# Order of TensorE's work over the last two batches of a cross-attention, causal self-attention and mixture-of-experts layer

## The chip, the cores and the metric

The kernel runs on 1 core of one Trainium2 chip. The metric is the device time of one execution in microseconds (us), median of several runs. Before the change it is 362.99 us (3 runs, 362.04 to 364.71).

## What is computed

One transformer layer in float32 over x of shape (4, 128, 512), that is 4 batches of 128 tokens, with a context of (4, 2048, 384). The reference, cut to its steps:

```
x = x + cross_attention(layernorm(x), ctx, Wq, bq, Wk, bk, Wv, bv)      # one head of 512
n = layernorm(x)
cq  = layernorm(n @ W_dq)  * g + b ;  Q = cq @ W_uq
ckv = layernorm(n @ W_dkv) * g + b ;  K, V = split(ckv @ W_ukv)
s = tril(Q K' / sqrt(32)), exact zeros become -inf                       # 16 heads of 32
x = x + softmax(s) V  W_o'
n = layernorm(x)
routed = sum over 4 of 16 experts of w_e * relu(n U_e')^2 D_e'
shared = relu(n SU')^2 SD'                                              # inner width 1024
x = x + routed + shared
```

## The kernel before

Everything is written out by hand, one instruction stream for each engine, tied by semaphores. The context is read in 16 chunks of 512 keys (4 for each batch), and the main loop goes over steps: scores of a chunk, its exponential, its transpose and its product with the context, each some steps behind the other. The later stages of a batch (attended values, the middle layer norm, the compressed queries and keys, the self-attention, the output projection) are woven into the steps of the batches behind it. After the last step comes a tail in which nothing of the chunk loop is left to lay between, written as a plain list of calls on each engine. The change is in TensorE's list there. The names in it:

- `sums_T(b)`, `attended(b)`: the cross-attention's result of batch b, transposed and multiplied with Wv.
- `rows_T(n, bank)` (L1589): four transposes of a normalised batch into a bank of PSUM. "middle" is the norm ahead of the self-attention, "last" the one ahead of the experts. ScalarE then copies the bank's rounded high part (`rows_hi`, L745), VectorE the rest (`rows_lo`, L1084), since each product is made of three rounded products (`split_mm`, L1582 to L1584). An instruction of it has 128x128 weights and as many columns as the other operand is wide.
- `compress(b)`, `compressed_T(b)` (L1773), `keys_and_queries(b)` (L1785), `values(b)` (L1791): the projections of the self-attention. Between the first two VectorE makes moments and a normalisation (`moments_2`, `normalise_2`, with the root on GpSimd, L620).
- `pair_scores(u)` (L1732): scores of units u and u+1. A unit is 4 heads of a batch; there are 16 units (`UNITS`), 4 for each batch. VectorE then masks and takes maxima (`find_masked`, `put_lowest`, `highest`: L1092, L1096, L1100), ScalarE takes the exponential (`unit_exp`, L852), VectorE inverts the sums, GpSimd scales (`unit_weights`, L627), `unit_T(u)` (L1742) transposes on TensorE, ScalarE copies out (`unit_copy`, L841), and `unit_sums(b)` (L1801) multiplies with the values of a batch. `hs_bank(u)` gives the bank of a unit's scores: from unit 8 on they are banks 6, 4 and 0 by turns, unit 13 being the last one in bank 0. `pair_scores(u)` waits until the exponential of unit u-2 has been taken.
- `project(b)`: the output projection of batch b. VectorE adds it (`self_added`, L1328) and the last norm follows. `router(b)`: the gate's 16 columns for a batch.
- `first_up(e, m)`: up product of shared block e (0 or 1), column half m, for the first two batches at once, by `up_half(e, 0, m)`: 12 instructions of 256 columns each. `half_bank(e, h)` says into which bank. ScalarE takes `relu_half(e, 0)` and `squared_half(e, 0)`, VectorE `gated_half(e, 0)`. `first_down(e, b)` are the down products. Afterwards `up_half(e, 1, m)` makes the up products of the last two batches, and `up(2, counts)` those of block 2, with `counts` (L1967 to L1971), the first product that needs the routing, between. `entries` (L1979) is the second.

The orders on the other engines that matter: ScalarE has `unit_exp(9)`, `attended_hi(1)`, `down_hi(0)`, `down_hi(1)`, `unit_exp(10)`, `compressed(3)` in this row, and at the end `unit_copy(15)`, `relu_half(0, 0)`, `attended_hi(3)`, `squared_half(0, 0)`, `rows_hi` of batch 2, `router_exp(2)`, `relu_half(1, 0)`. VectorE has `rows_lo` of batch 3, `find_masked(10)`, `put_lowest(10)`, `attended_lo(1)`, `moments_2(3)`. Then, after the last `rows_lo`, comes `down_lo(2)`, the routing (its selection is L1164), the gate weights (L1170 to L1183), and the table of entries (to L1215).

Of the kernel before, what the change touches and what calls it, by code (L numbers as in the profile page):

```python
# [25 lines left out]
P = 128  # L26
# [10 lines left out]
def layer_program(nc, x, ctx_in, ctxT_in, wqT, wkT, wv, wd, wu, woT, experts, bq, bk, bv, gate, bias_e,  # L37
                  gammas_betas, out):
    NB, S, D = x.shape
    NKEY, TD = ctx_in.shape[1:]  # L40
    DC = D // P
# [12 lines left out]
    IC = 2  # L54
# [24 lines left out]
    with ExitStack() as es:  # L79
# [38 lines left out]
        xT_h = sb("xT_h", [P, DC, T], F32R)  # L118
        xT_l = sb("xT_l", [P, DC, T], F32R)
# [110 lines left out]
        def u_part(e, i):  # L230

            return u_w[e][:, i, :]
# [48 lines left out]
        def small(name, shape, dt=F32):  # L281
# [36 lines left out]
        bank = [es.enter_context(nc.psum_tensor(f"bank{i}", [P, 512], F32)) for i in range(8)]  # L318
# [16 lines left out]
        var_ok, rstd_ok, xn_ok, xT_mm, xhi_ok, xlo_ok = (sem(n) for n in ("var_ok", "rstd_ok", "xn_ok", "xT_mm", "xhi_ok", "xlo_ok"))  # L335
# [7 lines left out]
        qkv_mm, qkv_ok, hs_mm, hnb_ok, exp_ok, hrd_ok, hw_ok, hwT_mm, hwT_ok, a_mm, ahi_ok, alo_ok, wo_mm, x2_ok = (sem(n) for n in (  # L343
            "qkv_mm", "qkv_ok", "hs_mm", "hnb_ok", "exp_ok", "hrd_ok", "hw_ok", "hwT_mm", "hwT_ok", "a_mm", "ahi_ok", "alo_ok", "wo_mm", "x2_ok"))
        lg_mm, rexp_ok, sel_ok, cnt_mm, cnt_ok, ent_ok, ent_mm, idx_ok = (sem(n) for n in (
            "lg_mm", "rexp_ok", "sel_ok", "cnt_mm", "cnt_ok", "ent_ok", "ent_mm", "idx_ok"))
        up_mm, relu_ok, sq_ok, g_ok, acc_mm, base_ok, y_out = (sem(n) for n in (
            "up_mm", "relu_ok", "sq_ok", "g_ok", "acc_mm", "base_ok", "y_out"))
# [10 lines left out]
        ulo_first, dlo_first = sem("ulo_first"), sem("dlo_first")  # L359
# [6 lines left out]
        def tok(b):  # L366
            return slice(b * S, (b + 1) * S)
# [10 lines left out]
        UNITS = NB * ROWS  # L378
# [3 lines left out]
        B_S, B_W, B_O, B_POST, B_A = 2, 3, 4, 5, 7  # L382


        B_ACC, B_UP = (1, B_O, B_A, B_S), ((B_POST, 0), (6, B_W))

        def rows_bank(b):

            return 1 if b < NB - 1 else B_S
# [8 lines left out]
        HT_TOK = T // 2  # L398
# [3 lines left out]

        def half_bank(e, h):

            return B_UP[e][0] if h else B_POST

        def half(h):
            return slice(h * HT_TOK, (h + 1) * HT_TOK)
# [34 lines left out]
        norm_no = {(kind, b): NB + i for i, (_, kind, b) in enumerate(order)}  # L443
# [1133 lines left out]
        def _(pe):  # L1577
            mm = nc.tensor.matmul

            def split_mm(dst, a, b, start, stop):  # L1580

                mm(dst, a[0], b[1], start=start, stop=False)  # L1582
                mm(dst, a[0], b[0], start=False, stop=False)  # L1583
                return mm(dst, a[1], b[0], start=False, stop=stop)  # L1584

            def rows_T(n, dst):
                pe.wait_ge(xn_ok, n + 1)
                for c in range(DC):
                    last = nc.tensor.transpose(dst[:, c * P:(c + 1) * P], xn[:, n % 2, c * P:(c + 1) * P], ident[:])  # L1589
                last.then_inc(xT_mm, 1)  # L1590
# [34 lines left out]
            for h in range(DC):  # L1625
                for i in range(2):
                    last = mm(bank[B_ROW][0:2, 0:TDB], bq2[:, h, :], wk2[:, i, h, :], start=h == 0 and i == 0, stop=h == DC - 1 and i == 1)
# [65 lines left out]
            def up_half(e, h, m):  # L1693
# [7 lines left out]
                if m == IC - 1:  # L1701
                    last.then_inc(up_mm, 1)

            def first_up(e, m):
                pe.wait_ge(xlo_ok, norm_no["last", 1] + 1)
                if e == 0:
                    pe.wait_ge(qkv_ok, 3 * NB - 1)
                else:
                    pe.wait_ge(relu_ok, e)
                up_half(e, 0, m)  # L1710

            def first_down(e, b):
                pe.wait_ge(dlo_first, 2 * e + 2)
                pe.wait_ge(g_ok, e + 1)
                if e == 0:
                    pe.wait_ge(rexp_ok, NB - 1)
                    pe.wait_ge(exp_ok, UNITS)
                down_tile(e, b, first=e == 0)

            def pair_scores(u):  # L1720

                b, r = divmod(u, ROWS)
                pe.wait_ge(qkv_ok, 3 * b + 2)
                if u > 2 * ROWS:
                    pe.wait_ge(exp_ok, u - 1)
                elif u >= 2:
                    pe.wait_ge(exp_ok, u)
                for j in range(HT):
                    for i in range(2):
                        rows = slice((r + i) * DH, (r + i + 1) * DH)  # L1730
                        o = slice(j * P, (j + 1) * P)
                        last = mm(bank[hs_bank(u + i)][:, o], qk_s[rows, 0, o], qk_s[rows, 1, o], start=True, stop=True)  # L1732
                last.then_inc(hs_mm, 2)

            def unit_T(u, step=TAIL):
                pe.wait_ge(hw_ok, u + 1)
                if step - LAG < G:
                    pe.wait_ge(wT_ok, step - LAG + 1)
                else:
                    pe.wait_ge(hwT_ok, u)  # L1740
                for j in range(HT):
                    last = nc.tensor.transpose(bank[B_W][:, j * P:(j + 1) * P], hw_of(u)[:, j * P:(j + 1) * P], ident[:])  # L1742
                last.then_inc(hwT_mm, 1)
# [49 lines left out]
            def unit_sums(b):  # L1793
                pe.wait_ge(hwT_ok, ROWS * b + ROWS)
                pe.wait_ge(qkv_ok, 3 * b + 3)
                if b >= 1:
                    pe.wait_ge(alo_ok, b)
                for j in range(HT):
                    for r in range(ROWS):
                        h = j * ROWS + r  # L1800
                        last = mm(bank[B_A][r * DH:(r + 1) * DH, j * P:(j + 1) * P], v_s[:, b % 2, h * DH:(h + 1) * DH],  # L1801
                                  hwT(b * ROWS + r)[:, j * P:(j + 1) * P], start=True, stop=True)
                last.then_inc(a_mm, 1)
# [15 lines left out]
            def router(b):  # L1819
                pe.wait_ge(xlo_ok, norm_no["last", b] + 1)  # L1820
                for c in range(DC):
                    last = split_mm(bank[rows_bank(b)][:, 0:NE], (xT_h[:, c, tok(b)], xT_l[:, c, tok(b)]),
                                    (gate_h[:, c, :], gate_l[:, c, :]), c == 0, c == DC - 1)
                last.then_inc(lg_mm, 1)
# [37 lines left out]
            for step in range(1, TAIL):  # L1862
# [22 lines left out]
                if 0 <= g < G:  # L1885
                    b, c = divmod(g, NCH)
# [22 lines left out]
            unit_T(6)  # L1909
            router(0)  # L1910
            unit_T(7)
            rows_T(norm_no["middle", 3], bank[B_POST])
            pair_scores(10)
            unit_sums(1)
            compress(3)
            project(1)
# [6 lines left out]
            unit_T(10)  # L1923
            pe.wait_ge(rexp_ok, 1)
            rows_T(norm_no["last", 1], bank[rows_bank(1)])
            pair_scores(14)
            unit_T(11)
            router(1)
            unit_sums(2)
            unit_T(12)  # L1930
            for m in range(IC):
                first_up(0, m)
            unit_T(13)
            project(2)
            unit_T(14)
            unit_T(15)
            unit_sums(3)
            rows_T(norm_no["last", 2], bank[rows_bank(2)])
            for m in range(IC):
                first_up(1, m)  # L1940
            project(3)
            router(2)
            first_down(0, 1)
            first_down(0, 0)
            rows_T(norm_no["last", 3], bank[rows_bank(3)])
            first_down(1, 1)
            router(3)
            first_down(1, 0)

            for e in range(FIRST):  # L1950
                pe.wait_ge(relu_ok, FIRST)
# [203 lines left out]
```

## Time and profile before

| | us |
|---|---|
| median of 3 runs | 362.99 (362.04 to 364.71) |
| the profiled execution | 367.77 |
| span of its trace | 366.0 |
| TensorE busy | 342.7 (94%) |
| VectorE busy | 241.0 (66%) |
| ScalarE busy | 189.1 (52%) |
| GpSimd busy | 94.9 (26%) |
| mean granted TensorE clock | 0.967 |

All starts in the text are in us from the start of the span. PE is TensorE's matmul, DVE VectorE, ACT ScalarE, POOL GpSimd. The clock is a share of full speed: 1.00 is 2.4 GHz, 0.50 is 1.2 GHz. The listed duration of a matmul overlaps with the next one's, so its price in a row of matmuls is the distance of two starts.

### The profile page before, as it was taken

What the parts mean: (1) busy time and instruction counts of PE and PEld (TensorE: products, weight loads), DVE (VectorE), ACT (ScalarE), POOL (GpSimd) and SP (SyncE); (2) the same over time, 40 slices, a digit from 0 to 9 for tenths busy, and PEclk for the clock granted to TensorE, in tenths of its full rate; (3) what the DMA queues carried; (4) which work ended last, traced back from release to release, by engine and by line L of the source; (5) the groups of instructions that cost most, each with busy time, mean ns of one, the idle gap of its engine ahead of it and who ended that gap; (6) DMA issues with size and microseconds to landing.
All of it is one profiled execution on the core that took longest, in us unless ns stands there. A gap on an engine that the chain in (4) does not pass through costs nothing.

```text
span 366.0 us, 6994 instructions
## 1 busy us (share of the span) xinstructions
PE 342.7 (94%) x2530; PEld 239.9 (66%) x2530; DVE 241.0 (66%) x475; ACT 189.1 (52%) x428; POOL 94.9 (26%) x114
## 2 busy tenths in 40 slices
PE   6999799999999989998879889999998999999996
PEld 4887567677677757766669779887643444444344
DVE  2875978746588377576782468880534677778587
ACT  2547574635566574484754452502134677777520
POOL 3600500000012011443472140004336554432000
PEclk9999999999999999996977998989999999999999
DMA  6982689976222345071050460699834453331573
GB/s 234 402 360 99 236 339 422 375 244 223 86 88 87 107 166 218 29 277 69 3 193 10 144 258 1 243 376 411 318 108 154 148 175 120 126 107 57 202 288 115
DMA packets 17185, 69.70 MB, mean 190 GB/s; under 512 B 2816, under 2 KB 3328, under 8 KB 14592
## 3 DMA queue, kind: packets, MB, share of 16 engines
q1 hardware_dynamic: 12768, 56.93, 41.4%
q0 software_dynamic: 3520, 11.54, 9.2%
q10 hardware_dynamic: 864, 0.79, 0.7%
q8 instruction: 21, 0.34, 0.4%
q14 instruction: 12, 0.10, 0.1%
HBM read 61.91 MB, written 7.34 MB: 189 GB/s over the span
## 4 chain that ended last, share of the span: by engine, by line
PE 74%; DVE 12%; ACT 6%; issue 3%; DMA 2%; another core or an unknown queue 1%; POOL 1%; ACTq 0%; DVEq 0%
PE bank L1582 9%; PE bank L2030 9%; PE bank L2062 9%; PE bank L1584 9%; PE bank L1583 9%; PE bank L1892 8%; PE bank L1999 2%; DMA raw<-in_wkT 2%; PE bank L2073 2%; PE bank L2041 2%; PE bank L1732 2%; DVE cT L1283 2%; PE bank L1785 2%; PE bank L1742 1%; PE bank L1837 1%
## 5 line engine op out<-in xcount | busy, mean ns | idle before, releaser
L1892 PE MATMUL bank<-ring,wT 128*128 128x384 f32 x128 | 44.0, 487 | 0.7 <-ACT wT L894 0.7
L2030 PE MATMUL bank<-WX,xsT 128*32 128x256 f32 (+1 forms) x256 | 38.0, 380 | 0.9 <-DVE xsT L1492 0.9
L2062 PE MATMUL bank<-WX,hsT 128*32 128x512 f32 (+1 forms) x128 | 38.2, 598 | 0.0
L1283 DVE TENSOR_TENSOR cT<-ring_T,cT 128x512 fp32r<-128x512 f32 x45 | 31.0, 732 | 6.6 <-ACT cT L752 6.6
L1892 PEld LDWEIGHTS bank<-ring,wT 128*128 128x128 f32 x128 | 23.6, 190 | 14.2 <-ACT wT L894 0.9
L2030 PEld LDWEIGHTS bank<-WX,xsT 128*32 128x32 f32 x256 | 17.8, 110 | 22.0 <-issue 11.9
L1514 DVE COPY down_copy<-WX 128x1024 f32 x32 | 21.0, 696 | 15.0 <-PE bank L2062 14.8
L2030 PE MATMUL bank<-up_copy,xsT 128*32 128x256 f32 x384 | 30.7, 379 | 0.0
L2062 PE MATMUL bank<-down_copy,hsT 128*32 128x512 f32 x192 | 30.7, 598 | 0.0
L752 ACT CAST cT<-ring_T 128x512 fp32r<-128x512 f32 x48 | 27.0, 618 | 6.5 <-PE bank L1584 6.3
L688 POOL DMA_INDIRECT xs<-x_rows,from_row x20 | 19.6, 982 | 40.7 <-DVE to_row L1237 27.3
L598 POOL TENSOR_TENSOR rstd<-var,mhalf 128x1 f32<-128x1 f32 x12 | 7.5, 625 | 75.0 <-DVE var L1069 74.9
L1507 DVE COPY up_copy<-WX 128x1024 f32 x32 | 21.1, 695 | 8.3 <-remote 3.2
L695 POOL DMA_INDIRECT y_rows<-ys,to_row x16 | 17.1, 1072 | 35.7 <-ACT ys L1000 35.7
L1024 ACT COPY down_copy<-WX 128x1024 f32 x16 | 16.8, 1051 | 18.2 <-PE bank L2062 18.2
L1492 DVE COPY xsT<-bank 128x512 f32<-128x512 f32 x20 | 13.7, 684 | 17.8 <-PE bank L1999 17.6
L1582 PE MATMUL bank<-cT,qk_h 128*128 128x512 f32 x48 | 20.2, 420 | 2.4 <-DVE cT L1283 1.7
L1584 PE MATMUL bank<-cT,qk_l 128*128 128x512 f32 x48 | 18.9, 393 | 0.0
L1583 PE MATMUL bank<-cT,qk_h 128*128 128x512 f32 x48 | 18.8, 392 | 0.0
L1016 ACT COPY up_copy<-WX 128x1024 f32 x16 | 16.7, 1044 | 4.1 <-remote 2.4
L2062 PEld LDWEIGHTS bank<-WX,hsT 128*32 128x32 f32 x128 | 7.4, 109 | 16.4 <-issue 16.4
L1582 PE MATMUL bank<-xT_l,u_w 128*128 128x256 f32 (+1 forms) x48 | 17.8, 370 | 0.0
(296 smaller groups left out, 901.3 us busy)
## 6 DMA issues: line engine op xcount, KB each, us to landing
WX<-in_experts SPq DMA_DIRECT2D x16, 1024.0 KB, 6.0
ring_T<-in_ctxT SPq DMA_DIRECT2D x16, 768.0 KB, 7.1
ring<-in_ctx SPq DMA_DIRECT2D x16, 768.0 KB, 5.2
WX<-y_rows SPq DMA_DIRECT2D x4, 1024.0 KB, 8.2
raw<-in_experts SPq DMA_DIRECT2D x3, 1024.0 KB, 5.0
raw<-in_wqT SPq DMA_DIRECT2D x4, 256.0 KB, 5.7
res<-in_x SPq DMA_DIRECT2D x4, 256.0 KB, 8.2
raw<-in_woT SPq DMA_DIRECT2D x1, 1024.0 KB, 4.8
```

Of the source, the lines that this page charges most:

```text
L688: nc.gpsimd.indirect_dma_start(out=xs[:, s % NXS, :], out_offset=None, in_=x_rows, in_offset=bass.IndirectOffsetOnAxis(ap=from_row[:, s:s ...
L695: nc.gpsimd.indirect_dma_start(out=y_rows, out_offset=bass.IndirectOffsetOnAxis(ap=to_row[:, s:s + 1], axis=0), in_=ys[:, s % NYS, :], in_ ...
L752: copy(cT[:, g % 2, 0, t, :], ring_T[:, g % RING_T, t, :]).then_inc(cThi_ok, 1)
L1283: V_.tensor_tensor(cT[:, g % 2, 1, t, :], ring_T[:, g % RING_T, t, :], f32(cT[:, g % 2, 0, t, :]), ALU.subtract).then_inc(cTlo_ok, 1)
L1507: V_.tensor_copy(up_copy[place(g, q)][:], WX[:, bass.ds(expert * (2 * HALF), HALF)]).then_inc(up_copied, 1)
L1514: V_.tensor_copy(down_copy[place(g, q)][:], WX[:, bass.ds(expert * (2 * HALF) + HALF, HALF)]).then_inc(down_copied, 1)
L1582: mm(dst, a[0], b[1], start=start, stop=False)
L1583: mm(dst, a[0], b[0], start=False, stop=False)
L1584: return mm(dst, a[1], b[0], start=False, stop=stop)
L1892: last = mm(bank[B_O][:, 0:TD], wT[:, g % 2, k * P:(k + 1) * P], ring[:, g % RING, k, :], start=(c == 0 and k == 0), stop=(c == NCH - 1 an ...
L2030: last = mm(bank[B_H[g % 2]][q * SLOT:(q + 1) * SLOT, 0:IC * P], xsT[:, g % 2, c * P + q * SLOT:c * P + (q + 1) * SLOT], w, start=c == 0, ...
L2062: last = mm(bank[B_Y[g % 2]][q * SLOT:(q + 1) * SLOT, :], hsT[:, g % 2, m * P + q * SLOT:m * P + (q + 1) * SLOT], w, start=m == 0, stop=m ...
```

## The change

In TensorE's tail list, and nowhere else:

1. `pair_scores(10)` stands ahead of `rows_T` of batch 3's middle norm.
2. The up products of shared block 0 for the first two batches are cut by batch. `up_rows(0, m, 0)` makes those of batch 0 alone, 12 instructions of 128 columns for each m, and stands between `rows_T` of batch 1's last norm and `pair_scores(14)`. `up_rows(0, m, 1)` stands where `first_up(0, m)` was.
3. `first_up(1, m)` goes into bank 0 (before: bank 5, shared with block 0, so that it waited for block 0's relu). It waits for the exponential of unit 13 instead. Its two halves stand behind `unit_T(14)` and behind `unit_T(15)`; before, both stood behind `rows_T` of batch 2's last norm.
4. `first_down(1, 0)` stands ahead of `router(3)`.

```diff
         def half_bank(e, h):
-            return B_UP[e][0] if h else B_POST
+            return B_UP[e][0] if h else B_UP[0][e]
...
+            def up_rows(e, m, b):
+                for c in range(DC):
+                    o = c * IC * P + m * P
+                    last = split_mm(bank[half_bank(e, 0)][:, m * HT_TOK + b * S:m * HT_TOK + (b + 1) * S],
+                                    (u_part(e, 0)[:, o:o + P], u_part(e, 1)[:, o:o + P]),
+                                    (xT_h[:, c, tok(b)], xT_l[:, c, tok(b)]), c == 0, c == DC - 1)
+                return last
+
             def first_up(e, m):
                 pe.wait_ge(xlo_ok, norm_no["last", 1] + 1)
-                if e == 0:
-                    pe.wait_ge(qkv_ok, 3 * NB - 1)
-                else:
-                    pe.wait_ge(relu_ok, e)
+                pe.wait_ge(exp_ok, UNITS - 2)
                 up_half(e, 0, m)
...
             unit_T(7)
+            pair_scores(10)
             rows_T(norm_no["middle", 3], bank[B_POST])
-            pair_scores(10)
             unit_sums(1)
...
             rows_T(norm_no["last", 1], bank[rows_bank(1)])
+            pe.wait_ge(ulo_first, 2)
+            pe.wait_ge(xlo_ok, norm_no["last", 0] + 1)
+            pe.wait_ge(qkv_ok, 3 * NB - 1)
+            for m in range(IC):
+                up_rows(0, m, 0)
             pair_scores(14)
             unit_T(11)
             router(1)
             unit_sums(2)
             unit_T(12)
+            pe.wait_ge(xlo_ok, norm_no["last", 1] + 1)
             for m in range(IC):
-                first_up(0, m)
+                last = up_rows(0, m, 1)
+            last.then_inc(up_mm, 1)
             unit_T(13)
             project(2)
             unit_T(14)
+            first_up(1, 0)
             unit_T(15)
+            first_up(1, 1)
             unit_sums(3)
             rows_T(norm_no["last", 2], bank[rows_bank(2)])
-            for m in range(IC):
-                first_up(1, m)
             project(3)
...
             first_down(1, 1)
+            first_down(1, 0)
             router(3)
-            first_down(1, 0)
```

The added lines move the line numbers behind them: L1732, L1742, L1801 of before are L1738, L1748, L1807 afterwards. First place, TensorE from `unit_T(7)` (L1742, L1748) to `unit_sums(1)` (L1801, L1807); L1589 is `rows_T` of batch 3, L1732 and L1738 are `pair_scores(10)`. Before:

```order
L1742 MATMUL bank<-ident,hw 128x128 x4
L1589 MATMUL bank<-ident,xn 128x128 x4
L1732 MATMUL bank<-qk_s 128x128 x8
L1801 MATMUL bank<-hwT_first,v_s 32x128
L1801 MATMUL bank<-hwT_odd,v_s 32x128
```

and now:

```order
L1748 MATMUL bank<-ident,hw 128x128 x4
L1738 MATMUL bank<-qk_s 128x128 x8
L1589 MATMUL bank<-ident,xn 128x128 x4
L1807 MATMUL bank<-hwT_first,v_s 32x128
L1807 MATMUL bank<-hwT_odd,v_s 32x128
```

The scores have passed the transposes that wait for VectorE's `xn`. Second place, TensorE from `unit_T(10)` to `unit_T(11)`; L1589 is `rows_T` of batch 1's last norm, L1732 and L1738 are `pair_scores(14)`, `u_w` is the up weight of shared block 0. Before:

```order
L1742 MATMUL bank<-ident,hw_more 128x128 x4
L1589 MATMUL bank<-ident,xn 128x128 x4
L1732 MATMUL bank<-qk_s 128x128 x8
L1742 MATMUL bank<-ident,hw_more 128x128 x4
L1582 MATMUL bank<-gate_l,xT_h 128x16
```

and now:

```order
L1748 MATMUL bank<-ident,hw_more 128x128 x4
L1589 MATMUL bank<-ident,xn 128x128 x4
L1582 MATMUL bank<-xT_l,u_w_72 128x128
L1583 MATMUL bank<-xT_h,u_w_72 128x128
L1584 MATMUL bank<-xT_h,u_w_72 128x128
...
L1738 MATMUL bank<-qk_s 128x128 x8
L1748 MATMUL bank<-ident,hw_more 128x128 x4
L1582 MATMUL bank<-gate_l,xT_h 128x16
```

Eight such triples, 24 instructions of 128 columns, now stand ahead of the last scores. Third place, TensorE from `project(2)` to `project(3)` in the changed kernel, with the banks' numbers: `unit_T(14)`, `first_up(1, 0)`, `unit_T(15)`, `first_up(1, 1)`, `unit_sums(3)`, `rows_T` of batch 2, `project(3)`, each by its first row. Now:

```order
L1748 MATMUL bank3<-ident,hw_more_84 128x128 x4
L1582 MATMUL bank0<-xT_l,u_w1_73 128x256
...
L1748 MATMUL bank3<-ident,hw_more_84 128x128 x4
L1582 MATMUL bank0<-xT_l,u_w1_73 128x256
...
L1807 MATMUL bank7<-hwT_last_68,v_s 32x128
...
L1589 MATMUL bank1<-ident,xn 128x128 x4
L1582 MATMUL bank2<-wo_w_61,aT_last_71 128x512
```

and before, from the same `unit_T(14)` on:

```order
L1742 MATMUL bank3<-ident,hw_more_84 128x128 x8
L1801 MATMUL bank7<-hwT_last_68,v_s 32x128
...
L1589 MATMUL bank1<-ident,xn 128x128 x4
L1582 MATMUL bank5<-xT_l,u_w1_73 128x256
...
L1582 MATMUL bank2<-wo_w_61,aT_last_71 128x512
```

The 24 products of block 1 have gone from between `rows_T` and `project(3)` to behind the two last transposes of units. The lists of the other engines are the same as before.

## Rows read from the trace of the kernel before

**Rows 1.** The page: granted TensorE clock in 40 slices of 9.15 us, in tenths.

```profile
PEclk9999999999999999996977998989999999999999
```

**Rows 2.** Waits of PE, 155 to 260 us: total, times, longest.

```profile
PE bank L1732 <- ACT hw_more L852: 2.4, 1, 2.4
PE bank L1589 <- DVE xn L1079: 1.5, 1, 1.5
...
PE bank L1742 <- ACT hwT_last L841: 0.8, 1, 0.8
PE bank L1582 <- DVE xT_l L1084: 0.7, 1, 0.7
PE bank L1801 <- ACT hwT_odd L841: 0.7, 1, 0.7
```

**Rows 3.** Timeline of PE, 166 to 178 us: start, duration, instruction, idle before.

```profile
166.43 0.92 PE L1589 MATMUL bank<-ident,xn 128*128 128x128 f32 x4 [1.51 <-DVE xn L1079]
167.28 2.08 PE L1732 MATMUL bank<-qk_s 32*128 32x128 f32 x16
169.29 0.42 PE L1801 MATMUL bank<-hwT_first,v_s 128*32 128x128 f32 x1
...
171.15 0.58 PE L1582 MATMUL bank<-DW,xT_h 128*128 128x256 f32 x1
...
176.51 0.44 PE L1773 MATMUL bank<-ident,cqn 128*128 128x128 f32 x2
177.85 2.05 PE L1785 MATMUL bank<-cf,wu_s 128*128 128x128 f32 x16 [0.90 <-ACT cf L861]
```

**Rows 4.** Timelines of ACT and of DVE, 163 to 175 us.

```profile
163.46 0.21 ACT L852 ACTIVATION_READ_ACCUMULATOR hw_more<-bank,hnb 128x1 f32 x1
...
168.00 0.69 DVE L1084 TENSOR_TENSOR xT_l<-bank,xT_h 128x512 fp32r<-128x512 f32 x1 [0.16 <-ACT xT_h L745]
...
173.92 0.50 DVE L1338 BATCH_NORM_STATS2 stats<-bank 128x6 f32<-128x128 f32 x2 [1.25 <-PE bank L1584]
```

**Rows 5.** Windows: stretch, length, busy PE, PEld, DVE, ACT, POOL; granted clock; DMA.

```profile
167.00:173.40 6.40, 6.40 (x60) 5.42 (x59) 3.64 (x7) 3.52 (x11) 2.27 (x2) 0.50 0.01 3
...
187.50:197.20 9.70, 9.70 (x73) 8.97 (x72) 5.40 (x10) 5.95 (x28) 4.08 (x4) 0.50 0.31 120
...
221.50:224.60 3.10, 3.10 (x15) 2.94 (x14) 2.79 (x16) 0.00 (x0) 0.00 (x0) 0.50 0.00 0
```

**Rows 6.** Timelines of PE (and one row of DVE, L1318), 186 to 212 us.

```profile
186.54 1.55 PE L1732 MATMUL bank<-qk_s 32*128 32x128 f32 x16 [2.38 <-ACT hw_more L852]
...
189.43 0.36 PE L1582 MATMUL bank<-gate_l,xT_h 128*128 128x16 f32 x1
189.64 0.36 PE L1583 MATMUL bank<-gate_h,xT_h 128*128 128x16 f32 x1
...
205.36 0.66 PE L1589 MATMUL bank<-ident,xn 128*128 128x128 f32 x4
...
206.12 0.69 DVE L1318 TENSOR_TENSOR aT_last<-bank,aT_last 128x512 fp32r<-128x512 f32 x1 [1.12 <-ACT aT_last L831]
...
206.10 0.28 PE L1584 MATMUL bank<-xT_h,u_w 128*128 128x256 f32 x1
206.21 0.28 PE L1582 MATMUL bank<-xT_l,u_w 128*128 128x256 f32 x1
...
211.59 0.26 PE L1584 MATMUL bank<-gate_h,xT_l 128*128 128x16 f32 x1
```

**Rows 7.** Timelines of PE and DVE, 211 to 242 us.

```profile
211.71 0.26 PE L1582 MATMUL bank<-gate_l,xT_h 128*128 128x16 f32 x1
...
227.35 0.20 DVE L1164 TENSOR_SCALAR r_sel<-r_rank 128x64 f32<-128x64 f32 x1
...
230.30 0.33 PE L1967 MATMUL bank<-r_sel,upper 128*128 128x64 f32 x2
...
239.93 0.48 DVE L1215 TENSOR_TENSOR in_group<-r_eq,cw 128x320 f32<-128x320 f32 x1
...
241.75 3.75 PE L1979 MATMUL bank<-in_group,in_row 128*128 128x40 f32 x32
```

## The prediction

> **What bounds the kernel now.** I read the table of busy times first. TensorE works 94% of the span and the next engine 66%, so time is won only where TensorE stands idle, runs at the low clock, or does less. The clock line of the page comes second [rows 1]: it is at full speed but for the slices from the 19th to the 27th (165 to 247 us), which is where the changed list runs. The waits of TensorE come third [rows 2]: in the tail it waits once for 2.4 us, once for 1.5, and three times for 0.7 to 0.8. The two long ones are the starts at 186.54 and 166.43 in the timeline [rows 6, 3]. The windows come fourth [rows 5]. From 167.0 to 173.4 and from 187.5 to 197.2 TensorE is busy all the time at clock 0.50, that is 1.2 GHz: the two low stretches follow the two long waits by less than a microsecond. A third, 221.5 to 224.6, follows the wait of 0.7 at `router(3)` and that router's instructions of 16 columns. So a wait here costs its own length and a few microseconds at half speed behind it.
>
> The chain of waits goes through VectorE, ScalarE and TensorE by turns until the last scores, and from `router(3)` at 218.84 on TensorE alone is on it. What TensorE gains ahead of that point, the end gains, unless VectorE's routing becomes late.
>
> **Part A, scores ahead of the transposes.** `rows_T` waits for VectorE's `xn` from 164.92 (166.43 less 1.51) on, and the scores of units 10 and 11 stand behind it. Their own condition was met at 163.67, when the exponential of unit 8 was done [rows 4], and their banks 0 and 6 are free with it. They cost 2.01 us at half speed (167.28 to 169.29) [rows 3], so 1.0 at full, and end at about 165.95 inside the wait; `rows_T` starts at 166.43 as before. The wait left is 0.5.
> If the clock falls again at the same place: `rows_T` 0.85, `unit_sums(1)` 1.86 (169.29 to 171.15), then `compress(3)` from 169.14 instead of 171.15. Its 12 instructions take 2.56 at 0.213 each and end at 171.7. `project(1)` behind it begins at half speed (0.46 each), with 3.8 of its 12 instructions before the clock rises at 173.45 and the others at 0.23, and ends at 175.35. `compressed_T` stood right behind `project(1)` at 176.51: 1.16 won. If the clock doesn't fall, `compress(3)` has to wait for `xT_l`, done at 168.69 [rows 4], ends at 170.1, and VectorE's `moments_2` starts some 3.3 earlier than its 173.92; `project(1)` needs VectorE's low part of the attended values, which comes near 170.6, and is done at 173.4: 3.1 won. The two ends are 1.2 and 3.1. Both have rows; I take 2.0. From `compressed_T` to the end of the exponential of unit 12 the chain goes through VectorE's list, which is unchanged and shifts as a whole, GpSimd's and ScalarE's parts with it.
>
> **Part B, the products around the last units**, counted in the times of before, from the end of `rows_T` at 184.16 (186.54 less 2.38) to the end of `project(3)` (208.68 and 12 x 0.232, 211.46).
> - The price of an instruction of 128 columns isn't in the trace. One of 16 columns starts 0.112 to 0.12 after the other at full clock (211.59 to 211.71) and one of 256 columns 0.11 to 0.12 (206.10 to 206.21); at half clock one of 16 takes 0.21 [rows 6, 7]. The width makes no difference between 16 and 256, so one of 128 should be 0.112 as well. The other bound is the float32 product that isn't made of rounded parts: 16 instructions of 128 columns for 8 products in 2.05, 0.256 for a product [rows 3]. I take 0.112, since the same kind of instruction stands on both sides of it. The Trainium skill says (TensorE: Matmul & The Clock Gate, "Step-by-step: what each phase is for") that the time to load the stationary operand scales with its columns and that the load runs beside the matmul ahead of it. By that rule the price is the load's, 0.112 as well, and the rows of 16 and 256 columns agree.
> - Cut by batch, 24 instructions of 256 columns (2.8) become 48 of 128 (5.4): 2.6 more work.
> - The first 24 take 2.7 and fill the wait of 2.38: −2.38, and the last scores come 0.3 late, which is in the 2.6.
> - `first_up(1, m)` fills the waits of 0.8 and 0.7 at `unit_T(15)` and `unit_sums(3)`: −1.45.
> - It no longer stands between `rows_T` of batch 2 and `project(3)`. That projection needs the low part of the attended values, which was there at 206.81, 1.45 after `unit_sums(3)` was through at 205.36 [rows 6]. With only `rows_T` (0.42) between, TensorE waits 1.0. Behind it stand router, down products, and all that follows. +1.0.
> - The clock. The low stretch lasts 10 us and costs half of it, 5. The wait in front of it is filled, but with narrow products, and what follows is the same scores of 32 rows, transposes, router and sums as before. Between 0 and 5, I take half, 2.5.
> Sum of B: 2.6 − 2.38 − 1.45 + 1.0 − 2.5 = −2.7. With bounds of 0 and 5 for the clock it is −0.2 to −5.2.
> The transposes stand in a rule that speaks against the change: the Trainium skill says ("Part 4: PE-mode transpose" of the same page) that transposes don't count as work for the clock as matmuls do. The trace can't separate them, but the stretch from 187.5 to 197.2, TensorE all busy with 16 transposes among it and the clock at 0.50, goes with the rule. By it the clock term is nearer 0 and the sum of B near −0.2.
>
> **Part C, `first_down(1, 0)` ahead of `router(3)`.** The down products cover the wait of 0.7 for `xT_l` [rows 2]: −0.7. The low stretch behind (221.3 to 224.7, 1.7 lost) [rows 5] may go with it: 0 to 1.7, I take 1.0. What is late next is VectorE: its selection was ready at 227.55 and used at 230.30, 2.75 to spare, and the tables for `entries` at 240.41 against 241.75, 1.34 to spare [rows 7]. The router's result reaches VectorE 1.4 later in TensorE's row than before, so the spare 1.34 is used up, and TensorE waits 0 to 0.5 at `entries`: +0.2. Sum of C: −1.5, bounds 0 and −2.4.
>
> **Edits at nothing.** Bank 0 for block 1 waits for the exponential of unit 13, some 6 us before its use; if that came late, `unit_T(15)` and the sums would stand behind it. Loads of the routed experts hang on TensorE's milestones (`hwT_mm`, `wo_mm`, `up_mm`, `acc_mm`) and move with them. ScalarE's and GpSimd's lists are unchanged and hold waits of several microseconds.
>
> **Sum.** 2.0 + 2.7 + 1.5 = 6.2 us off the profiled execution's 367.77 gives 361.6. That execution is 4.8 above the median of 362.99, so against the median it is 356.8.
>
> **Rivals.**
> 1. *The clock holds through the whole tail.* A 3.1, B 5.2, C 2.4: 10.7 off, 352.3. For it: the two long waits are the plainest thing in front of the two low stretches. Against it: what runs there stays narrow.
> 2. *The clock is no better.* A 1.2, B 0.2, C 0.7: 2.1 to 3 off, 360.4. For it: TensorE was busy all of 187.5 to 197.2 and the clock still didn't rise for 10 us; against it, the wait of 2.38 is gone.
> 3. *Narrow products are dear.* At 0.256 each the 48 cost 12.3 in place of 2.8: 9.5 more, not 2.6. That takes 6.9 from the gain: 363.7, no change. For it: the 128-column row of 0.128 an instruction; against it, that is another mode, and 16 columns cost 0.112.
> 4. *The products ahead of the last scores hold up the unit chain at low clock: slower.* If the clock is already down when `up_rows(0, m, 0)` starts, its 24 instructions take 24 x 0.213 = 5.1 and `pair_scores(14)` starts 2.7 late. Masks, exponentials, `unit_T(13)` to `unit_T(15)` and `project(2)` follow it. The second 24 take 5.1 against 4.3, `project(2)` at half speed 5.6 against 2.8, and the wait of 1.0 stays: 2.7 + 0.8 + 2.8 + 1.0 − 1.45 = 5.9 more, less the 1.2 of A: 367.7. It decides from where the 24 take longer than 2.4 plus what A gives, 0.15 each. Against it: before, the clock was at 1.00 until after 186.54.
>
> **How the numbers follow.** The sum as it stands 0.48, rival 1 0.15, rival 2 0.22, rival 3 0.09, rival 4 0.06. The median of this kernel can be told from another to about 1%, 3.6 us. Faster by over that (below 359.4) are rival 1, nearly all of the forecast and a third of rival 2: 0.72. Within it: the rest of these and rival 3, 0.22. Slower: 0.06. The range leaves out rival 4, most of rival 3 and the far end of rival 1: 352.0 to 361.8. The time is the forecast's, 356.8.
>
> **What would show it.** In the profile after: `rows_T` with a wait of 0.5 instead of 1.5 and `compressed_T` 1 to 3 us earlier; no wait of 2.4 ahead of the last scores; instructions of 128 columns 0.112 apart; a new wait of about 1 us at `project(3)` for the low part of batch 3 (L1318); no wait at `router(3)`; fewer microseconds at clock 0.50 between 165 and 225. The prediction is wrong if the 128-column instructions stand 0.2 or more apart at full clock, if the low stretches are as long as before, or if TensorE waits over 1 us for the routing or the tables.

## The result, and the profile after

The changed kernel takes 355.44 us (4 runs, 354.00 to 355.67), the one before 363.85 beside it (4 runs, 362.04 to 365.23). The ratio is 0.974, with a 95% interval of 0.971 to 0.978: faster by 2.6%, 8.4 us. Forecast were 356.8 us with a range of 352.0 to 361.8.

| us | before | after |
|---|---|---|
| profiled execution | 367.77 | 355.39 |
| its span | 366.0 | 353.7 |
| TensorE busy | 342.7 (94%) | 336.4 (95%) |
| mean granted clock | 0.967 | 0.990 |

TensorE now has 24 more matmuls and is busy 6.3 us less. The clock line of the page [rows 1] says why:

```profile
PEclk9899999999999999999899999999999999999999
```

TensorE runs fewer microseconds at half speed. In the tail one slice below full speed is left, the 20th (8, from 168 to 177 us; the windows put the low stretch at 166 to 170). The 8 in the second slice is 3.4 us at half speed between 9 and 13 us, which the trace before doesn't have. The waits of TensorE between 155 and 255 us, in total, times, longest:

```profile
PE bank L1791 <- ACT cf L861: 0.9, 1, 0.9
PE bank L1582 <- issue: 0.9, 1, 0.9
PE bank L1582 <- ACT r_exp L878: 0.5, 1, 0.5
...
PE bank L1589 <- DVE xn L1079: 0.3, 1, 0.3
...
PE bank L1582 <- DVE r_pos L1203: 0.2, 1, 0.2
```

Of [rows 2], the wait of 2.4 is gone, the one of 1.5 is 0.3, and the three of 0.7 to 0.8 are gone. New are 0.9 at L1582, which is `project(3)`, and 0.2 at `down_half(0)`, the first down products that need the row numbers which VectorE makes from the routing (L1203).

Part A in the timeline of TensorE, which answers to [rows 3]:

```profile
164.99 0.63 PE L1748 MATMUL bank<-ident,hw 128*128 128x128 f32 x4 [0.26 <-ACT hwT_first L841]
165.55 1.27 PE L1738 MATMUL bank<-qk_s 32*128 32x128 f32 x16
167.12 1.12 PE L1589 MATMUL bank<-ident,xn 128*128 128x128 f32 x4 [0.30 <-DVE xn L1079]
...
169.99 0.38 PE L1582 MATMUL bank<-DW,xT_h 128*128 128x256 f32 x1
...
174.65 0.38 PE L1779 MATMUL bank<-ident,cqn 128*128 128x128 f32 x2
```

The scores (L1738) stand in the wait. From `unit_T(7)` to `compressed_T` it is 9.66 us (164.99 to 174.65) where it was 12.21 (164.30 to 176.51). The transposes and sums behind still ran at half clock: 32 sums from 168.17 to 169.99 take 1.82, before 1.86. The first row of `compress(3)`, at 169.99, is at full clock again.

Part B. The windows of the changed kernel (stretch, length, busy PE, PEld, DVE, ACT, POOL, granted clock, DMA), against [rows 5]:

```profile
165.00:170.00 5.00, 4.70 (x57) 3.48 (x57) 4.44 (x7) 2.31 (x9) 3.17 (x4) 0.66 0.37 156
...
181.00:185.00 4.00, 4.00 (x35) 3.78 (x36) 3.86 (x9) 2.93 (x12) 3.94 (x4) 1.00 0.44 123
185.00:188.50 3.50, 3.50 (x60) 3.36 (x62) 2.63 (x4) 2.08 (x11) 2.33 (x3) 1.00 0.61 245
188.50:192.00 3.50, 3.50 (x42) 3.30 (x35) 2.88 (x6) 3.29 (x17) 1.40 (x2) 1.00 0.42 146
192.00:200.00 8.00, 8.00 (x82) 7.13 (x81) 2.45 (x6) 2.90 (x9) 2.88 (x4) 1.00 0.17 56
```

From 181 to 200 us TensorE is busy without a gap and the clock is 1.00 all the time. The stretch of 10 us at 0.50 is gone. The prices in its timeline, with [rows 6]:

```profile
181.64 0.60 PE L1589 MATMUL bank<-ident,xn 128*128 128x128 f32 x4
182.00 0.31 PE L1582 MATMUL bank<-xT_l,u_w 128*128 128x128 f32 x1
182.14 0.27 PE L1583 MATMUL bank<-xT_h,u_w 128*128 128x128 f32 x1
182.25 0.28 PE L1584 MATMUL bank<-xT_h,u_w 128*128 128x128 f32 x1
...
184.80 1.16 PE L1738 MATMUL bank<-qk_s 32*128 32x128 f32 x16
...
199.87 0.66 PE L1589 MATMUL bank<-ident,xn 128*128 128x128 f32 x4
201.42 0.47 PE L1582 MATMUL bank<-wo_w,aT_last 128*128 128x512 f32 x1 [0.89 <-issue]
```

An instruction of 128 columns starts 0.11 after the other. The 24 of them take 2.80 (182.00 to 184.80), with a slower first and last step; the 22 steps from 182.14 to 184.60 are 0.112 each. `project(3)` waits 0.89. The profile names no releaser, but its condition is in VectorE's timeline: the low part of batch 3, 200.63 to 201.32, 0.1 ahead of the start.

```profile
200.63 0.69 DVE L1318 TENSOR_TENSOR aT_last<-bank,aT_last 128x512 fp32r<-128x512 f32 x1 [2.26 <-ACT aT_last L831]
```

Part C and what follows: from the end of `project(3)` to `entries` it was 30.29 us (211.46 to 241.75). In the profile after it is 28.27 (204.27 to 232.54), and the clock is 1.00 in all of it. The tables that `entries` reads (L1215) are ready at 232.31, only 0.2 before.

The traces differ by 12.3 us of span, the medians by 8.4. The profiled execution before was 3.9 above its median, so the sum over the traces is too large, and the medians decide. Of the 12.3, 3.1 lie behind the start of `entries`, where nothing was changed (124.25 us to the end before, 121.16 after). The trace before has a fourth low stretch there, and a wait of 0.9 for VectorE (`xsT`, L1492) that the trace after lacks:

```profile
245.00:249.00 4.00, 4.00 (x14) 3.23 (x14) 1.18 (x9) 0.00 (x0) 1.22 (x2) 0.57 1.01 422
```

### The profile page after: what moved, and what is told of

Same layout as the page of the kernel before. It is cut to its first block, busy times and chain, and to the rows that moved or that the text cites. A ratio compares the mean times of both kernels' runs of the same rounds, so it can differ in the third digit from the quotient of the medians.

```text
span 353.7 us, 7041 instructions
## 1 busy us (share of the span) xinstructions
PE 336.4 (95%) x2554; PEld 235.2 (67%) x2554; DVE 240.7 (68%) x475; ACT 189.4 (54%) x428; POOL 95.6 (27%) x114
## 4 chain that ended last, share of the span: by engine, by line
PE 76%; DVE 12%; ACT 6%; issue 3%; DMA 2%; POOL 0%; ACTq 0%; DVEq 0%
PE bank L2075 10%; PE bank L2043 10%; PE bank L1582 8%; PE bank L1898 8%; PE bank L1584 8%; PE bank L1583 8%; PE bank L2012 3%; PE bank L1791 2%; PE bank L2054 2%; PE bank L2086 2%; DMA raw<-in_wkT 2%; DVE cT L1283 2%; PE bank L1748 2%; PE bank L1843 2%; PE bank L1589 1%
## 5 line engine op out<-in xcount | busy, mean ns | idle before, releaser
L2043 PEld LDWEIGHTS bank<-WX,xsT 128*32 128x32 f32 x256 | 17.9, 110 | 21.0 <-issue 10.7
L1492 DVE COPY xsT<-bank 128x512 f32<-128x512 f32 x20 | 13.7, 685 | 14.8 <-PE bank L2012 14.8
L1582 PE MATMUL bank<-cT,qk_h 128*128 128x512 f32 x48 | 20.2, 420 | 2.4 <-DVE cT L1283 1.7
L1582 PE MATMUL bank<-xT_l,u_w 128*128 128x256 f32 (+2 forms) x56 | 17.9, 320 | 0.0
```

The costliest lines, as they stand in the source:

```text
L2043: last = mm(bank[B_H[g % 2]][q * SLOT:(q + 1) * SLOT, 0:IC * P], xsT[:, g % 2, c * P + q * SLOT:c * P + (q + 1) * SLOT], w, start=c == 0, ...
```

## The experiments

Each is timed beside the kernel before on its chip (364.8 in the first two groups, 363.0 in the third), so I compare by the ratio to it and by the difference of the medians.

**One part at a time.** `e1_scores_first` is the kernel before with part A alone:

```diff
+            pair_scores(10)
             rows_T(norm_no["middle", 3], bank[B_POST])
-            pair_scores(10)
```

> Part A alone: pair_scores(10) ahead of rows_T of batch 3, nothing else. Theory (the parts add up, as the trace after reads): about 2.5 us faster than before, 361.3, with compressed_T some 9.7 us behind unit_T(7) instead of 12.2. Rival (part A is given back because the later wait of 2.4 us and the low clock behind it stay): under 1 us, no change.

Measured: 360.22 us, ratio 0.987 (0.984 to 0.991), 4.5 us faster. That is more than the 2.5 of the theory (the interval is 3.3 to 5.9 us), and the rival is out. `compressed_T` starts 9.22 behind `unit_T(7)`, near the 9.7 named. The clock goes further with it: in this trace it was 1.00 throughout part A, and the low stretch at the units lasted 6.8 us instead of 10.2.

`e2_products` is the changed kernel with `rows_T` ahead of `pair_scores(10)` and `router(3)` ahead of `first_down(1, 0)` as before, so part B alone.

```diff
-            pair_scores(10)
             rows_T(norm_no["middle", 3], bank[B_POST])
+            pair_scores(10)
...
-            first_down(1, 0)
             router(3)
+            first_down(1, 0)
```

> Part B alone: the up products of block 0 cut by batch and laid ahead of the last scores, block 1 in bank 0. Theory: 5.3 us from rows_T of batch 1 to the end of project(3) as in the trace after, so 4.5 to 6 us faster than before. Rival (the clock stays full there only because part A has moved everything): the low stretch stays, and the gain is 0.2 to 2.7 us.

Measured: 359.0 us, ratio 0.985 (0.980 to 0.989), 5.8 us faster, as the theory says. The windows show the low stretch of part A as before and none at the units:

```profile
166.60:173.40 6.80, 6.73 (x61) 5.70 (x62) 4.28 (x8) 3.52 (x11) 2.27 (x2) 0.53 0.00 0
184.00:188.00 4.00, 4.00 (x44) 3.85 (x42) 3.82 (x8) 2.51 (x11) 3.96 (x4) 1.00 0.64 184
188.00:199.00 11.00, 11.00 (x111) 10.20 (x109) 6.72 (x13) 7.00 (x30) 4.88 (x5) 1.00 0.28 102
```

So part B holds the clock by itself, without part A's help.

`e3_down_first` is the kernel before with part C alone.

```diff
+            first_down(1, 0)
             router(3)
-            first_down(1, 0)
```

> Part C alone: first_down(1, 0) ahead of router(3). Theory: 0.7 us for the wait it covers and up to 1.7 for the low stretch behind it: 0.7 to 2 us faster. Rival (VectorE's routing is what the end hangs on): 0 or slower, with TensorE waiting for the tables instead.

Measured: 362.77 us, ratio 0.994 (0.990 to 0.998), 2.0 us faster and clear of zero, at the upper end of the theory's range. In its trace the low stretch behind `router(3)` is gone.

The three single gains, 4.5, 5.8 and 2.0, add to 12.3, where the whole change gives 8.4 (7.8 in the third group). The traces show where they overlap. Each row gives one trace's distances between four starts of TensorE and the end of the span, and in brackets how many of these microseconds were at a clock of 0.50 (without the last 5 us, where TensorE is mostly idle):

| us | `unit_T(7)` to `compressed_T` | `rows_T` of batch 1 to `router(2)` | `router(2)` to `entries` | `entries` to the end |
|---|---|---|---|---|
| before | 12.21 (6.8) | 27.90 (10.2) | 30.29 (3.4) | 124.25 (3.4) |
| part A, e1 | 9.22 (0) | 26.01 (6.8) | 30.26 (3.4) | 122.59 (3.4) |
| part B, e2 | 12.21 (6.8) | 22.60 (0) | 28.77 (0) | 122.64 (3.4) |
| part C, e3 | 11.85 (6.8) | 27.88 (10.2) | 28.27 (0) | 121.08 (0) |
| all, after | 9.66 (3.4) | 22.63 (0) | 28.27 (0) | 121.16 (0) |

Part A alone also won 1.9 us in B's stretch, and part B alone 1.5 in C's stretch, by low stretches that were shorter or absent. In the whole change such a microsecond can be won only once. With no low stretch behind the router, part C's order is worth 0.5 (28.77 less 28.27), the wait of 0.7 less the new 0.24.

**The clock by itself.** `e4_idle_filled` moves nothing. It only lays 20 products that nobody reads into the wait of 2.4 us of the kernel before:

```diff
             rows_T(norm_no["last", 1], bank[rows_bank(1)])
+            pe.wait_ge(xlo_ok, norm_no["last", 0] + 1)
+            pe.wait_ge(qkv_ok, 3 * NB - 1)
+            for _ in range(20):
+                mm(bank[B_POST][:, 0:2 * P], u_part(0, 0)[:, 0:P], u_part(0, 0)[:, 0:2 * P], start=True, stop=True)
             pair_scores(14)
```

> The kernel before with 20 products of 256 columns that nobody reads, laid into its wait of 2.4 us ahead of pair_scores(14): more work for TensorE, nothing moved. Theory (the clock is a large part of B): the stretch at clock 0.50 from 187.5 to 197.2 is gone or much shorter and the kernel is 2 to 5 us faster, though it does more. Rival (the clock is no better, rival 2 of the prediction): no change, 0 to 0.5 us slower.

Measured: 358.79 us, ratio 0.984 (0.981 to 0.988), 6.0 us faster with more work. In its windows the low stretch at the units is gone, and B's stretch is 23.25 us instead of 27.90: 4.65 for the clock alone. (The low stretches in part A and behind the router are shorter or gone in this trace too.)

```profile
181.00:185.00 4.00, 4.00 (x31) 3.30 (x30) 3.85 (x7) 2.64 (x11) 3.06 (x4) 1.00 0.29 84
185.00:188.50 3.50, 3.50 (x44) 3.19 (x46) 3.35 (x7) 2.53 (x10) 3.36 (x3) 1.00 0.73 281
188.50:192.00 3.50, 3.50 (x55) 3.30 (x48) 3.02 (x7) 3.28 (x16) 1.04 (x1) 1.00 0.49 154
```

`e8_idle_narrow` is e4's kernel with 16 columns instead of 256 in these 20 products.

```diff
-                mm(bank[B_POST][:, 0:2 * P], u_part(0, 0)[:, 0:P], u_part(0, 0)[:, 0:2 * P], start=True, stop=True)
+                mm(bank[B_POST][:, 0:NE], u_part(0, 0)[:, 0:P], u_part(0, 0)[:, 0:NE], start=True, stop=True)
```

> The kernel before with 20 products of 16 columns that nobody reads in the wait of 2.4 us: TensorE is as long occupied (0.112 each) as with the 20 of 256 columns, but the instructions are narrow. Theory (narrow instructions, like the router's, do not hold the clock): the low stretch stays and the time is that of the kernel before, 0 to 0.5 us more. Rival (any instruction in the wait holds the clock): 2 to 6 us faster, as with the wide ones (358.8).

Measured: 364.83 us, ratio 1.000 (0.997 to 1.003): nothing. The same 20 instructions are there for nearly as long, the wait of 2.4 has gone from its list of waits, and still the clock falls. First the timeline of e8, then, in the second fence, that of e4 (the count of L1732 is 14 and 10 of its 16, for the rows end with the window):

```profile
183.74 2.38 PE L1929 MATMUL bank<-u_w 128*128 128x16 f32 x20
186.19 1.05 PE L1732 MATMUL bank<-qk_s 32*128 32x128 f32 x14
```

```profile
182.75 2.63 PE L1929 MATMUL bank<-u_w 128*128 128x256 f32 x20
185.38 0.82 PE L1732 MATMUL bank<-qk_s 32*128 32x128 f32 x10
```

and the windows of e8:

```profile
185.00:188.50 3.50, 3.42 (x34) 3.24 (x34) 3.35 (x7) 2.36 (x10) 3.50 (x4) 0.88 0.77 268
188.50:192.00 3.50, 3.50 (x42) 3.27 (x41) 2.81 (x6) 1.83 (x10) 1.71 (x2) 0.50 0.52 167
```

From 188.5 to 192 TensorE is busy 3.50 of 3.50 us at clock 0.50 here and at clock 1.00 in e4, with the same real work in the row. What stood in the wait decides: 20 products of 256 columns kept the clock, 20 of 16 didn't. The low stretch lasts 6.8 us in e8's trace (187 to 195), shorter than the 10.2 before, but that execution is the fastest of e8's eleven, and the medians are equal.

`e9_both_filled` fills both long waits of the kernel before with such products, 12 more ahead of `rows_T` of batch 3:

```diff
+            pe.wait_ge(u_hi, 1)
+            for _ in range(12):
+                mm(bank[0][:, 0:2 * P], u_part(0, 0)[:, 0:P], u_part(0, 0)[:, 0:2 * P], start=True, stop=True)
             rows_T(norm_no["middle", 3], bank[B_POST])
```

> The kernel before with products that nobody reads in both long waits: 12 of 256 columns ahead of rows_T of batch 3 and 20 ahead of pair_scores(14). Nothing is moved, nothing left out. Theory (most of the change's gain is the clock's): no low stretch between 160 and 200 in most executions, and a time of 356 to 358.5, at most 3 us behind the changed kernel. Rival (the first low stretch comes from the narrow work after the wait, whatever stands in it): as with the second wait alone filled, 358.8.

Measured: 357.18 us, ratio 0.983 (0.978 to 0.987), 5.9 us faster, where the changed kernel in the same group is 7.8 faster. The windows show the clock at 1.00 from 167 to 199; a low stretch of 3.4 us behind `router(3)` (213 to 217) is left:

```profile
167.00:170.30 3.30, 3.30 (x59) 2.81 (x58) 3.11 (x7) 2.81 (x11) 2.10 (x2) 1.00 0.00 0
170.50:181.00 10.50, 9.35 (x67) 7.39 (x67) 8.03 (x21) 8.03 (x25) 5.23 (x7) 1.00 0.01 2
181.00:188.00 7.00, 7.00 (x92) 6.53 (x90) 6.36 (x13) 4.80 (x22) 5.87 (x6) 1.00 0.55 194
188.00:199.00 11.00, 9.56 (x93) 8.34 (x92) 5.21 (x12) 6.85 (x24) 4.10 (x5) 1.00 0.28 90
```

About three quarters of the gain can so be had without moving any work. The ratios of e4 and e9 can't be told apart, so whether the first wait adds to the second isn't shown by the times.

**Does the fill hold the clock in the changed kernel too?** `e5_wait_open` has its 24 products of batch 0 behind `unit_T(11)` instead of ahead of the last scores:

```diff
             rows_T(norm_no["last", 1], bank[rows_bank(1)])
-            pe.wait_ge(ulo_first, 2)
-            pe.wait_ge(xlo_ok, norm_no["last", 0] + 1)
-            pe.wait_ge(qkv_ok, 3 * NB - 1)
-            for m in range(IC):
-                up_rows(0, m, 0)
             pair_scores(14)
             unit_T(11)
+            pe.wait_ge(ulo_first, 2)
+            pe.wait_ge(xlo_ok, norm_no["last", 0] + 1)
+            pe.wait_ge(qkv_ok, 3 * NB - 1)
+            for m in range(IC):
+                up_rows(0, m, 0)
```

> The changed kernel with the 24 products of batch 0 moved from ahead of the last scores to behind unit_T(11): same instructions, the wait of 2.4 us open again. Theory (filling this wait is what holds the clock at full through the units): a low stretch of 7 to 10 us stands behind the wait again, mean clock 0.97 to 0.98, and 3 to 6 us are lost against the changed kernel, 358.5 to 361.5. Rival (the clock holds because block 1 and the rest are moved): only the wait is lost, 0 to 1 us, as the products fill nothing else but are needed anyway: about 356.

Measured: 359.24 us, ratio 0.987 (0.981 to 0.993), 3.8 above the changed kernel, and all five executions are above all nine of the changed kernel. That one wasn't timed beside it: by the differences to the kernel before the loss is 2.3 to 2.9. Its wait and windows:

```profile
PE bank L1738 <- ACT hw_more L852: 2.1, 1, 2.1
```

```profile
185.00:188.50 3.50, 3.50 (x24) 3.50 (x22) 2.99 (x6) 1.99 (x9) 2.41 (x3) 0.65 0.56 212
188.50:192.00 3.50, 3.50 (x18) 3.50 (x17) 1.21 (x2) 0.00 (x0) 0.28 (x1) 0.50 0.25 88
192.00:200.00 8.00, 8.00 (x72) 7.29 (x72) 1.05 (x3) 4.64 (x20) 2.08 (x2) 0.73 0.01 2
```

A wait of 2.1 is back, and a low stretch of 10.2 us behind it. The rival, 356, is out. Its five executions lie at 358.4 to 359.2 with a mean clock of 0.986 to 0.990 and at 361.7 and 362.0 with 0.981, so the low stretch isn't equally long in all of them.

`e6_uncut` is the changed kernel with nothing in that wait and block 0 uncut at its old place:

```diff
-            pe.wait_ge(ulo_first, 2)
-            pe.wait_ge(xlo_ok, norm_no["last", 0] + 1)
-            pe.wait_ge(qkv_ok, 3 * NB - 1)
-            for m in range(IC):
-                up_rows(0, m, 0)
             pair_scores(14)
...
             pe.wait_ge(xlo_ok, norm_no["last", 1] + 1)
+            pe.wait_ge(qkv_ok, 3 * NB - 1)
             for m in range(IC):
-                last = up_rows(0, m, 1)
-            last.then_inc(up_mm, 1)
+                up_half(0, 0, m)
```

> The changed kernel with block 0's products uncut, 24 of 256 columns at their old place, and nothing in the wait of 2.4 us; block 1 in bank 0 and the other edits stay. Theory: 2.7 us less work than the cut one, but the wait and the low stretch are back: 357.5 to 360.5. Rival (the wait's length is what counts, not the clock): wait 2.4 back, work 2.6 gone: 355.2, no difference from the changed kernel.

Measured: 357.33 us, ratio 0.981 (0.976 to 0.986), 1.9 above the changed kernel's 355.44; just under the theory's range, but above all of the changed kernel's executions. That one wasn't timed beside it: by the differences to the kernel before it is 0.3 to 1.0, and the intervals of the ratios overlap. The traces put the place: B's stretch takes 25.43 us here and 22.63 in the changed kernel, with the wait of 2.1 and 6.8 us at clock 0.50 against 2.6 us less work. So cutting block 0 and filling the wait with it is worth 0.3 to 2 us net, much less than what the filled wait and the clock give by themselves. Cutting without filling costs 1.9 (e5 less e6), less than the 2.6 us of added work.

`e10_without_c` is the changed kernel with part C undone:

```diff
-            first_down(1, 0)
             router(3)
+            first_down(1, 0)
```

> The changed kernel with router(3) ahead of first_down(1, 0) again, as before. Theory (part C is a wait of 0.7 and a low stretch behind it in some executions): 0.7 to 2.4 us slower than the changed kernel, 356.2 to 357.9. Rival (VectorE's row numbers bound this part, so the router's earlier result pays for the wait): the same, and no wait of 0.24 at down_half(0).

> The changed kernel as it is, beside the others on one chip. All theories: 355 to 356; it is there as the measure for e10 and e12.

Measured: 357.87 us without part C and 355.27 for the changed kernel beside it (`e11_change_again` is that kernel unaltered; ratios 0.983 and 0.977). Part C is worth 2.6 us at the medians. Two of the five executions of e10 reach clock 0.995 and take 355.4 and 356.2; the other three have 0.986 and take 357.9 to 358.3. The trace of e10 is the one of 355.4 and has no low stretch behind the router; C's stretch takes 28.77 in it, 0.5 more than in the changed kernel. That the slower three have that low stretch is likely by their mean clock and by e3, but they have no trace. The 0.24 at `down_half(0)` isn't among the waits of e10's trace as listed, in line with the rival's mechanism, but the time speaks against the rival.

**A version that goes further.** `e7_better`, and `e12_better_again` beside e11, fill the new wait at `project(3)` and lift a wait that bank 4 doesn't need:

```diff
-            first_up(1, 1)
+            up_half(1, 0, 1, 0)
             unit_sums(3)
             rows_T(norm_no["last", 2], bank[rows_bank(2)])
+            up_half(1, 0, 1, 1)
...
                 if e == 0:
-                    pe.wait_ge(rexp_ok, NB - 1)
+                    if b == 0:
+                        pe.wait_ge(rexp_ok, NB - 1)
```

(The fourth argument of `up_half` takes the first or the second two of the four row blocks.)

> The changed kernel with two more edits: the last 6 products of first_up(1, 1) stand behind rows_T of batch 2, in the new wait of 0.9 us at project(3), and first_down(0, 1), whose bank holds no logits, no longer waits for the router's exponential (0.48). Theory (TensorE alone is on the path from there): 0.7 + 0.4 = 1.1 us faster than the changed kernel, 354.3. Rival (the gain is given back where down_half(0) waits for VectorE's row numbers, 0.24 us already): under 0.5 us.

> The changed kernel with the two edits of e7_better, beside the changed kernel. Theory: 0.8 to 1.5 us faster than it. Rival (the first comparison was the chip's and the day's): under 0.5 us.

Measured: 353.91 us (ratio 0.971, 0.966 to 0.976), and 354.58 against 355.27 for the changed kernel (ratios 0.975 and 0.977, intervals that overlap): 0.7 faster, a little less than the 0.8 to 1.5 expected. In the trace of e7 the wait of 0.89 is 0.18, and the down products (L1582, `d_w`) start without one:

```profile
199.98 0.47 PE L1582 MATMUL bank<-wo_w,aT_last 128*128 128x512 f32 x1 [0.18 <-issue]
...
204.09 0.48 PE L1582 MATMUL bank<-d_w,gh 128*128 128x512 f32 x1
```

The first edit is worth 0.67 by the traces: B's stretch takes 21.96 instead of 22.63. The second won nothing: `router(2)` to `entries` takes 28.25 where it was 28.27, since 0.3 of the lifted 0.48 comes back as a wait for `xn` (L1079), and TensorE still waits 0.2 for the row numbers (L1203). That was the rival's mechanism. The rest of e7's lead is the clock in part A, which its edits don't touch and which was 1.00 there in this execution.

Over all ten executions this version takes 353.6 to 355.9 us, median 353.95; the nine of the changed kernel take 354.0 to 355.7, median 355.4. It is faster by 1.4 us by these and by 0.7 beside each other, and the two ranges overlap, so a gain of about 0.7 is likely but not clear of noise.

## Why the prediction was right, and where its sizes were off

The time lay in the range and the mechanism holds: the waits were filled and the clock behind them rose. By its own steps:

- **Part A**, forecast 2.0 between 1.2 and 3.1: in the trace 2.55 between the same two instructions, with the clock low for `rows_T` and the sums as in the branch of 1.2 and up again for `compress(3)`. The wait left is 0.30, not 0.5. In the traces of e1, e7 and e10 the clock stayed at 1.00 there, and 2.99 to 3.02 were won, the other branch's 3.1. So both branches occur from one execution to the next, and the middle value was a bet between them.
- **The price of 128 columns**, forecast 0.112: 0.112. The bound of 0.256 is out, and rival 3 with it.
- **Filled waits**, −2.38 and −1.45: both are gone from the list.
- **The new wait at `project(3)`**, forecast 1.0, for L1318: 0.89, for L1318.
- **The clock term of part B** is the term that was mis-sized. It was put at 2.5, half of what the low stretch cost, for want of anything that told 0 from 5. The trace has B at 5.27 (183.56 to 211.46 before, 27.90; 181.64 to 204.27 after, 22.63) where the sum had 2.7, and the clock is 1.00 throughout. With the other terms as forecast, 5.1 are left for the clock: the term is the whole 5. e4, which wins by the clock alone, has 4.65 in the same stretch; in times e4 and e2 are 6.0 and 5.8 us faster.
- **Part C**, forecast 1.5: 2.02 in the trace, 2.0 in e3 and 2.6 in e10 against e11; 0.5 of it is the order, the rest the low stretch behind the router, which was put at 1.0 and gave 1.5. The late routing was foreseen at `entries`, 0 to 0.5; it came as 0.24 at `down_half(0)`, for the row numbers.
- **The sum**, 6.2 forecast, 8.4 measured. In the traces the three parts won 9.8, so the sum was 3.6 too small there, while the time is off by 1.4. That is partly luck. The trace after reaches the changed rows 0.7 later than the one before (164.99 against 164.30). And the sum, read in one execution's trace, was set against the median by a fixed 4.8; beside the changed kernel the median was 363.85, so it was 3.9. The low stretch from 245 to 249 us, in the prediction's own 27th slice, got no term.
- **The rivals.** Rival 1 (the clock holds through the whole tail, 352.3) came nearer in its mechanism, 10.7 against the 9.8, than in its time. Rival 2 is out by e4 against e8. Rival 3 is out by the 0.112; its price of 0.256 was also read from listed durations, and by the distance of starts (177.85 to 179.74 in the trace before) it was 0.236. Rival 4 is out by the start of the last scores right behind the products at 184.80, at full clock.
- **The chances.** Those of the three cases below 359.4, as given, add to 0.70 and not to 0.72.
- The step that argued with the transposes and the Trainium skill's rule on them ("Part 4: PE-mode transpose" of TensorE: Matmul & The Clock Gate) for a clock term near 0 didn't hold as it was used. The stretch from 187.5 to 197.2 has 8 transposes in it, not 16 (4 at 188.02 and 4 at 193.29), and the same 8 ran at clock 1.00 in the changed kernel (185.89 and 188.73). Whether a transpose counts for the clock isn't shown by that; e8 tests instructions of 16 columns, not transposes.

## What to carry to other kernels

Where a stretch runs at half clock although TensorE is busy in it, look at what stands in front: a wait, or narrow instructions. Here 20 useless products of 256 columns in one wait gave 6.0 us. That is also the quickest test: lay wide products that nobody reads into the wait, and only if the time falls look for real work to put there. Count what the real work costs there: the filled wait was worth 0.3 to 2 us net here (e6), since block 0 had to be cut for it at 2.6 us. Gains that come by the clock don't add, so parts have to be timed together.

## What the runs showed of the hardware that was not expected

- TensorE occupied without a gap isn't enough for the clock. With 20 instructions of 16 columns in the wait (2.38 us long in the timeline) the clock still fell, and the kernel took 364.83 us beside 364.76 without them; with 20 of 256 columns (2.63 us) it held and the kernel took 358.79 beside 364.77.
- One kernel's executions fall into groups by the clock. The 15 of the kernel before in the second group of runs have mean clocks of 0.962 to 0.976: at 0.976 they take 362.5 to 363.1 us, at 0.967 364.7 to 365.2. Most of the scatter goes with how much low clock an execution has. It doesn't explain all: two of the 15 (365.97 at 0.972, 366.95 at 0.962) lie outside these groups or between them, and the profiled execution took 367.77 at 0.967.
- A product of 128 columns with 128x128 weights costs what one of 16 or 256 does, 0.11 to 0.12 us apart at full clock, so halving the width of 256 doubles the price of the work. That was the forecast, and no row of the kernel before had shown it for 128.
